# GpSimd sums 24 probability tiles in six groups of four instead of eight groups

## What is computed

```python
attn = jnp.einsum('bnhd,bmhd->bhnm', q * scale, k)
attn = jax.nn.softmax(attn + bias[None], axis=-1)
out = jnp.einsum('bhnm,bmhd->bnhd', attn, v).reshape(Bw, Nw, Cd)
return out @ proj_w + proj_b
```

## Time and profile before

| | us |
|---|---|
| median of 3 runs | 7109.32 |
| lowest, highest | 7107.28, 7114.14 |
| the profiled execution, its time | 7105.39 |
| its span | 7103.7 |

### The profile page before, as it was taken

One profiled execution on the slowest core, in us unless ns is written; L12 is line 12 of the kernel. 1 busy time (PEld: TensorE's weight loads), 2 busy tenths in 40 slices (PEclk: granted clock), 3 DMA queues, 4 the chain that ended last, 5 costly groups with the idle time before them and its releaser, 6 DMA issues. The chain is left out here.

```text
span 7103.7 us, 127413 instructions
## 1 busy us (share of the span) xinstructions
PE 6266.2 (88%) x39184; PEld 3733.0 (53%) x39184; DVE 4906.7 (69%) x9450; ACT 3283.0 (46%) x6693; POOL 4197.0 (59%) x1309
## 2 busy tenths in 40 slices
PE   3777687779999999999999999999999975429999
PEld 2666554545555555555555555555555534316666
DVE  2666533367777777777777777777777738777661
ACT  1444311126666666666666666666666650002222
POOL 0222222248888888888888888888888874400000
PEclk9999899969999999999999999999999997769999
DMA  1111144431001101101101101101100003431110
GB/s 41 42 43 44 52 149 159 160 86 42 26 22 39 30 22 32 37 22 32 37 22 32 37 22 32 37 22 31 36 16 15 17 23 113 94 42 44 39 36 28
DMA packets 217938, 329.21 MB, mean 46 GB/s; under 512 B 53026, under 2 KB 179634, under 8 KB 213938
## 3 DMA queue, kind: packets, MB, share of 16 engines
q1 hardware_dynamic: 214794, 320.56, 16.4%
q10 hardware_dynamic: 2664, 2.62, 0.2%
HBM read 191.84 MB, written 130.88 MB: 45 GB/s over the span
## 5 line engine op out<-in xcount | busy, mean ns | idle before, releaser
L1191 DVE TENSOR_REDUCE tops<-ps_m 128x1 f32<-128x448 f32 (+1 forms) x5600 | 3116.8, 616 | 910.4 <-PE ps_m L1094 860.1
L1167 ACT ACTIVATE prob<-ps_s 128x448 f32<-128x448 f32 (+1 forms) x5600 | 2613.3, 548 | 1751.0 <-PE ps_s L1030 1709.8
L1030 PE MATMUL ps_s<-queries,keys 97*128 97x448 f32 (+1 forms) x5600 | 2197.5, 397 | 15.2 <-ACT prob L1167 7.6
L1000 POOL TENSOR_TENSOR tile_sum<-prob 128x1792 f32<-128x1792 f32 x448 | 1803.0, 4024 | 660.3 <-ACT prob L1167 660.0
L1094 PE MATMUL ps_m<-keys,queries 96*128 96x448 f32 (+1 forms) x5600 | 2090.3, 380 | 35.9 <-DMA keys<-k_parts 20.3
L1000 POOL TENSOR_TENSOR tile_sum<-tile_sum,prob 128x1792 f32<-128x1792 f32 x448 | 1807.7, 4035 | 31.8
L1030 PEld LDWEIGHTS ps_s<-queries,keys 97*128 97x128 f32 (+1 forms) x5600 | 1041.6, 187 | 1156.5 <-ACT prob L1167 661.1
L1046 PE MATMUL ps_o<-prob,values 128*32 128x448 f32 x11200 | 1342.8, 551 | 2.9 <-ACT prob L1167 1.1
L1094 PEld LDWEIGHTS ps_m<-keys,queries 96*128 96x128 f32 (+1 forms) x5600 | 1061.7, 190 | 240.7 <-DVE tops L1191 84.3
L255 POOL TENSOR_TENSOR logit<-logit,top 112x896 f32<-112x896 f32 x112 | 188.4, 1682 | 556.6 <-DVE top L372 556.6
L1565 PE MATMUL ps_y<-w_down,hT 128*112 128x256 f32 x1792 | 396.0, 382 | 107.3 <-DVE y L1632 85.5
(11 more groups left out here) (122 smaller groups left out, 4441.1 us busy)
## 6 DMA issues: line engine op xcount, KB each, us to landing
queries<-q_parts SPq DMA_DIRECT2D x288, 160.0 KB, 3.3
keys<-k_parts SPq DMA_DIRECT2D x96, 392.0 KB, 6.8
xT<-in_x SPq DMA_DIRECT2D x56, 224.0 KB, 2.5
window_out<-oT SPq DMA_DIRECT2D x56, 224.0 KB, 2.0
aT<-window_out SPq DMA_DIRECT2D x56, 224.0 KB, 3.8
hidden<-h SPq DMA_DIRECT2D x28, 448.0 KB, 4.6
q_parts<-hi SPq DMA_DIRECT2D x56, 224.0 KB, 1.9
q_parts<-lo SPq DMA_DIRECT2D x56, 224.0 KB, 2.0
```

What stands on the lines that cost most here:

```text
L1000: nc.gpsimd.tensor_tensor(tile_sum[k % 2][:, :, :], left, prob[:, t % SLOTS, :, :], ALU.add).then_inc(summed, 1)
L1030: mm = nc.tensor.matmul(o[:, 0:CH], keys[x.u][:, j, at:at + k], queries[x.v][:, j, own:own + CH], start=True, stop=not last, skip_group_ch ...
L1167: nc.scalar.activation(prob[0:k, t % SLOTS, j, :], ps_s[0:k, score_bank(x.hm, i), 0:CH], ACT.Exp).then_inc(exp_done, 1)
L1191: nc.vector.tensor_reduce(tops[0:rows, j, r - blocks[0], c:c + 1], ps_m[0:rows, e % MB, 0:CH], AX.X, ALU.max).then_inc(m_used, 1)
```

## The change

The 24 full tiles are summed in six groups of four, (1, 2, 3, 4) to (21, 22, 23, 24), instead of (1, 2, 3, 4), six groups of three, and (23, 24). Per half GpSimd does 18 adds instead of 16, and TensorE 7 totals instead of 9 (tile 0's among them). The places of the totals follow from the groups' last tiles: tiles 7, 11, 15, 19, 23 and tile 2 of the next half, where they were 7, 10, 13, 16, 19, 22, and 0 and 2 of the next half. `NORMALIZE_AT` must be a tile that is added as the second or later of its group; it goes from 21 to 22, the second tile of the last group.

```diff
-SUM_TILES = [(1, 2, 3, 4)] + [(t, t + 1, t + 2) for t in range(5, 23, 3)] + [(23, 24)]
+SUM_TILES = [tuple(range(t, t + 4)) for t in range(1, KT, 4)]
...
-        NORMALIZE_AT = 21
+        NORMALIZE_AT = 22
```

## The result

The changed kernel takes 7208.28 us (median of 4 runs, 7198.95 to 7209.87) against 7111.07 before: ratio 1.0134, interval 1.0117 to 1.0152. Slower by 97 us. The forecast was slower, 7128; the direction and the place were right, the size was not. The profiled execution took 7198.95 us, 93.6 more than that of before.

A forecast was written before the change was run, and what follows sets the result against it. TensorE sets the pace (795 of 800 us busy), GpSimd next at 85%. Terms -83.1 saved, +92.9 waits, +8.6 last half give +18.4; from 7109.3 the forecast is 7128 us, range 7105 to 7150.

The forecast's parts named there:

- The saving: TensorE's path in the attention: two totals less per half at 0.755 us each, 83.1 us saved over 55 halves.
- GpSimd's lateness: GpSimd's chains of adds in the 98-fill halves: 12.20 us per group leaves it 2.32 us late at the sixth.
- The shift rows behind the store: SP's queue: normalisation 5.06 us later, 2.0 to spare; rows land 12.84 us after tile 22's first score, wanted at 9.80.
- The waits: TensorE's third score of the next half waits for shift rows, up to 3.04 us each, 92.9 us in all.
- The last half: Final half without fills, where GpSimd sets the time: 18 adds take 74.2 us instead of 65.6, 8.6 more.
- The price of a stop: TensorE's wait at the third score was costed at its length alone, 3.04 us, with granted clock 1.00.
- The rows come in time: Rival: shift rows land some 3 us sooner, only the last group's sum holds TensorE up; 7081 us, chance 0.08.
- Nothing waits: Rival: TensorE meets no new waits, only the totals saved and the longer final half count; 7035 us, chance 0.03.
- GpSimd slower: Rival: one VectorE instruction holds up an add in each group, 106 us more, over 7230 us; chance 0.02.
- the port rule: VectorE and GpSimd share an exclusively locked SBUF port pair; more GpSimd work would bring blocking and time above the sum.
- Query loads: SP's loads behind the shift rows: later too, costed at nothing; with no cover 2 us in 24 halves.

The follow-up runs named there:

- the turned order: Changed kernel with SP issuing the second pair of shift rows ahead of the store instead of behind it; 7107.54 us, ratio 1.0001 to the kernel before.

## Why the prediction was wrong in size

Point by point, by its own steps.

- *The saving*, 0.755 us per total and 83.1 in all: right. In the kernels without waits each half is 1.5 us shorter, whatever its fills.
- *GpSimd's lateness*, 2.32 us at the sixth group: right, 2.40.
- *The shift rows behind the store*: right, and the core of the case. 9.90 us to the end of the normalisation was 9.98, 0.68 to the issue was 0.68, 2.26 to the landing was 2.36 to 2.44 in the loop. The prediction called its 2.26 a case with no store ahead; its own rows have a store 4.5 us ahead of it. And the store's packets are not what makes 2.4 of 2.26: behind the loop of the changed kernel the store is issued 0.41 us ahead, and ten such waits still end 2.26 to 2.27 us after the issue. What the loop adds is open.

```profile
5684.46 0.37 SPq L925 DMA_DIRECT2D attention_out<-out  x1
5684.87 1.19 SPq L920 DMA_DIRECT2D queries<-shift_rows  x2
...
5687.14 0.42 PE L1030 MATMUL ps_s<-queries,keys 97*64 97x448 f32 x1 [1.33 <-DMA queries<-shift_rows]
```

- *The waits*, 92.9 us: right within 8%. 43 stops add up to 97.9 us, and the last half's to 2.0.
- *The last half*, 8.6 us more: 9.3. From its first add at 5849.97 to the last total at 5924.91 it takes 74.9 us, where 65.6 were measured before and 74.2 forecast. Counted from tile 2's first score it is 9.6 us more, which is the entry in the ledger below.

```profile
5849.97 4.00 POOL L1000 TENSOR_TENSOR tile_sum<-prob 128x1792 f32<-128x1792 f32 x1 [3.19 <-ACT prob L1167]
...
5924.91 1.72 PE L1058 MATMUL ps_d<-tile_sum,ones 128*32 128x448 f32 x8 [7.19 <-POOL tile_sum L1000]
```

- **The price of a stop was the step that failed.** "TensorE waits 3.04 us" stood for a cost of 3.04 us. Behind the 43 stops of the changed kernel another 54.0 us are lost, in tiles 0 and 1, where the granted clock is 0.50, the lower of TensorE's two levels, 1.2 in place of 2.4 GHz. With 3.0 behind the last half's stop that is 57 us of the 80 between forecast and result. The trace's record of the clock agrees with this count, which was made from tile lengths: ahead of the last half the clock stands at 0.50 for 126 us in 33 stretches, against 10 us in two before, and half of the 116 us more is 58. The Trainium skill (TensorE: Matmul & The Clock Gate, Part 1: The HAM clock gate) describes this: the lower clock is the resting state, activity releases it, and idling brings it back; the trace agrees, 0.50 in the rows from 3426 on and 1.00 from 3430.
- It could have been seen. At the loop's turn TensorE had stood still in the kernel before too, and behind it the stage row is not 1.00:

```profile
2692.00:2693.00 1.00, 0.56 (x3) 0.50 (x4) 0.00 (x0) 0.11 (x1) 0.85 (x1) 1.00 1.01 301
2694.00:2695.00 1.00, 1.00 (x6) 0.26 (x9) 1.00 (x3) 0.82 (x2) 0.00 (x0) 0.50 1.00 215
2696.00:2697.00 1.00, 1.00 (x12) 0.19 (x4) 0.57 (x1) 0.00 (x0) 0.00 (x0) 0.50 0.88 259
```

A mean over 800 us read 1.00 and hid it. Priced with hindsight at 1.3 to 1.6 us for each of some 35 long stops, the forecast would have been about 7174 to 7184, still short of 7208; the waits were 7 us longer than summed as well, and the ledger below has the rest.

- *The rivals.* "The rows come in time" (7081) is what one gets by moving the normalisation to tile 20, at 7092 with a few slow stretches. "Nothing waits" (7035) was reached at 7029 to 7035 with the totals one tile later. "GpSimd slower" fell: the adds are 4.03 us throughout, even at 98% of GpSimd's time. The prediction had used the port rule of the Trainium skill (SBUF — State Buffer, Who interferes with whom) against the change without its exception: the same section says that `tensor_reduce` on trn2 never contends with GpSimd, and the row maxima, tensor reduces, are 578 of VectorE's 623 us in the stretch of the earlier trace rows. So the adds' steady 4.03 us agrees with the page and doesn't test its lock.
- *Query loads*, costed at nothing: right for the changed kernel (five small waits, 2.1 us), but they were the next in the queue, as the turned order showed with 38 us.

The ledger of the profiled execution: -83.1 saved, +97.9 stops, +54.0 clock, +5.0 for the last half's own stop and clock, +9.6 last half; 83.4 us. The two profiles differ by 93.3. Of the other 10, 5.1 lie ahead of the attention, where nothing was changed, 1.2 behind it, and some 3.6 I can't place. That the part ahead of the attention moves by a few microseconds is seen in the other kernels as well: its first score stands at 1548 us here, at 1543 before and at 1540 to 1545 there.

What stays open is what decides, at a stop of 2 to 2.5 us, whether the clock falls. I did not look for it beyond these runs.

## What to carry to other kernels

When a step is moved, follow everything that is queued behind it on every engine it passes, to the first wait that has the least time to spare; here a single late normalisation went over a store to two rows of 512 numbers that TensorE needed. Price a stop of the pacing TensorE by more than its length: several half-clock microseconds may follow. And an engine at 98% is no loss by itself: groups of four gain 1% once the normalisation and the totals stand where the longer chain can't reach them.

## What the runs showed of the hardware

- A stop of TensorE of 1.4 us or more could be followed by a stretch at granted clock 0.50, in which eight weighing products take 1.72 us in place of 0.96. In most cases behind stops under 3.3 us it cost about 1.6 us, behind longer ones 1.6 to 3. Two stops of 2.45 and 2.48 us fell on different sides; behind all 54 stops over 3.3 us the clock fell.
- The product that waits for two transfers of shift rows, 2 KB each, starts 2.36 to 2.44 us after the first is issued in the loop and 2.26 to 2.27 behind it, both with a store of 224 KB issued 0.4 to 0.5 us ahead, and 2.26 with the store 4.5 us ahead. No cost of the burst in front is seen.
- GpSimd's adds of 128 x 1792 elements keep 4.03 us with VectorE busy 80% beside them and with hardly a gap between adds.
